# Expert attention: the next unit's keys projected right behind its queries, and rotated in front of the maxima of query tiles 2 and 3

## The reference

```python
q = (h @ wq + bq)   # 16 heads of 128; k and v likewise
q = q * cos + _rotate_half(q) * sin
k = k * cos + _rotate_half(k) * sin
scores = jnp.einsum('bhqd,bhkd->bhqk', q, k) / math.sqrt(HD)
scores = jnp.where(causal[None, None], scores, jnp.finfo(jnp.float32).min)
probs = jax.nn.softmax(scores.astype(jnp.float32), axis=-1).astype(q.dtype)
out = jnp.einsum('bhqk,bhkd->bhqd', probs, v)
```

## Time and profile before

| | |
|---|---|
| median of 3 runs | 2938.88 us (2935.98 to 2939.38) |
| the profiled execution | 2939.69 us |
| its span | 2937.9 us |
| mean granted TensorE clock | 0.93 |
| PE busy | 2447.8 us, 83% |
| DVE, ACT, POOL busy | 59%, 40%, 35% |

### The profile page before, as it was taken

One profiled execution on the slowest core, in us unless ns is written; L12 is line 12 of the kernel. 1 busy time (PEld: TensorE's weight loads), 2 busy tenths in 40 slices (PEclk: granted clock), 3 DMA queues, 4 the chain that ended last, 5 costly groups with the idle time before them and its releaser, 6 DMA issues. The chain is left out here.

```text
span 2937.9 us, 50913 instructions
## 1 busy us (share of the span) xinstructions
PE 2447.8 (83%) x18448; PEld 1669.7 (57%) x18448; DVE 1730.1 (59%) x3474; ACT 1184.5 (40%) x2881; POOL 1014.7 (35%) x1265
## 2 busy tenths in 40 slices
PE   6878778787787887878864999998979949999989
PEld 3467644676446774456742666667533336666675
DVE  4756667566685666846644766661356537666613
ACT  3643345344454434444422444440224514444401
POOL 0266521666215562146531444440040014444400
PEclk8999989999899998999977999999989979999989
DMA  2100001000010000000003000000010040000000
GB/s 49 40 2 2 2 15 33 2 2 2 8 36 5 2 2 8 18 6 2 2 1 102 17 16 16 11 5 1 2 42 1 1 102 18 16 16 11 5 0 15
DMA packets 74983, 46.64 MB, mean 16 GB/s; under 512 B 27416, under 2 KB 68256, under 8 KB 74400
## 3 DMA queue, kind: packets, MB, share of 16 engines
q1 hardware_dynamic: 74784, 43.95, 5.4%
HBM read 42.89 MB, written 1.05 MB: 15 GB/s over the span
## 5 line engine op out<-in xcount | busy, mean ns | idle before, releaser
L975 DVE SCALAR_TENSOR_TENSOR work<-four,taps_g,work 128x511 f32<-128x511 f32 (+2 forms) x384 | 284.2, 747 | 99.4 <-ACT work L751 89.2
L1365 POOL TENSOR_TENSOR rot<-q_plain,ropes 128x512 f32<-128x512 f32 x66 | 83.6, 1266 | 704.9 <-ACT q_plain L1387 704.9
L547 PE MATMUL four<-xT,wring 128*128 128x512 f32 x512 | 262.3, 640 | 11.9 <-issue 7.0
L1336 DVE TENSOR_REDUCE nmaxf<-four 128x1 f32<-128x512 f32 (+3 forms) x256 | 125.7, 491 | 165.5 <-PE four L1262 157.5
L1405 ACT ACTIVATE pr<-four,nmaxf 128x512 f32<-128x512 f32 (+3 forms) x256 | 133.9, 525 | 176.7 <-DVE nmaxf L1336 173.8
L1260 PE MATMUL four<-rot,rot 128*128 128x512 f32 (+3 forms) x512 | 189.7, 466 | 10.8 <-ACT oT L1200 5.6
L901 POOL TENSOR_TENSOR work<-work 128x256 f32<-128x256 f32 x184 | 120.3, 654 | 183.2 <-PE bank L634 91.4
L1368 POOL TENSOR_TENSOR rpart<-q_plain,ropes 64x512 f32<-64x512 f32 x132 | 167.3, 1268 | 10.3
L751 ACT ACTIVATE work<-four,taps_g 128x512 f32<-128x512 f32 x128 | 88.0, 688 | 187.9 <-PE four L547 187.9
L547 PEld LDWEIGHTS four<-xT,wring 128*128 128x128 f32 x512 | 99.6, 207 | 101.9 <-issue 95.7
L1281 PE MATMUL bank<-pT,vv 128*128 128x512 f32 (+3 forms) x512 | 149.4, 435 | 5.4 <-ACT pT L1411 5.4
(11 more groups left out here) (277 smaller groups left out, 5707.6 us busy)
## 6 DMA issues: line engine op xcount, KB each, us to landing
wqkv<-in_f_wq_dram SPq DMA_DIRECT2D x34, 128.0 KB, 2.2
wqkv<-in_f_wk_dram SPq DMA_DIRECT2D x34, 128.0 KB, 2.3
wqkv<-in_f_wv_dram SPq DMA_DIRECT2D x34, 128.0 KB, 2.3
wo<-in_f_wo_dram SPq DMA_DIRECT2D x2, 2048.0 KB, 11.3
we<-in_f_we_dram SPq DMA_DIRECT2D x4, 1024.0 KB
wring<-in_Ww_dram SPq DMA_DIRECT2D x4, 512.0 KB, 4.1
wring<-in_Wk_dram SPq DMA_DIRECT2D x4, 512.0 KB, 3.8
wring<-in_Wv_dram SPq DMA_DIRECT2D x4, 512.0 KB, 3.8
```

What stands on the lines that cost most here:

```text
L547: last = nc.tensor.matmul(k.bank[i % 3][:], wring[n % 2][:, c, h * P:(h + 1) * P], k.xT[:, c, b * T:(b + 1) * T], start=(c == 0), stop=(c ...
L975: ins = nc.vector.scalar_tensor_tensor(out=cbuf[i % 4][:, s:], in0=k.bank[i % 3][:, 0:T - s], scalar=taps_g[:, {"q": 0, "k": 1}.get(kind, ...
L1336: nc.vector.tensor_reduce(nmax[:, n:n + 1], k.bank[2 + i % 2][:, 0:(qt + 1) * P], AX.X, ALU.max, negate=True).then_inc(s_max, 1)
```

## The change

Three engines get another order inside a unit. On PE the key projection of the next unit moves from behind score tile 2 to directly behind the query projection. On DVE the rotation of those keys moves in front of maximum 2, and maximum 3 comes before scaling 2. On ACT the copies of turned tiles 0 and 1 move in front of exponentials 2 and 3. No instruction is added, taken away or resized, and the semaphores and the values waited for are the same.

```diff
@@ tensor engine, one unit
                             scores(u, 0)
                             scores(u, 1)
                             project(g, u + 1, 0)
+                            project(g, u + 1, 1)
                             scores(u, 2)
-                            project(g, u + 1, 1)
                             scores(u, 3)
@@ vector engine
                             maximum(u, 1)
                             normalise(u, 0)
                             normalise(u, 1)
+                            rope_k(g, u + 1)
                             maximum(u, 2)
+                            maximum(u, 3)
                             normalise(u, 2)
-                            maximum(u, 3)
-                            rope_k(g, u + 1)
                             normalise(u, 3)
@@ scalar engine
                             exps(u, 0)
                             exps(u, 1)
                             keep_q(g, u + 1)
+                            keep_p(u, 0)
+                            keep_p(u, 1)
                             exps(u, 2)
                             exps(u, 3)
-                            keep_p(u, 0)
-                            keep_p(u, 1)
```

## The result

The changed kernel takes 2957.66 us in the median (2954.47 to 2959.06, 4 runs), against 2939.13 us for the kernel before in the same session. The ratio is 1.0064, with a 95% interval of 1.0047 to 1.0081: 18.5 us slower. The forecast was 2948 us, 8.8 us slower, with a range of 2928 to 2965. Direction and mechanism held; the amount forecast was half of what came, and the time lies 1.7 us above the band of 2942 to 2956 that the forecast had given itself.

A forecast was written before the change was run, and what follows sets the result against it. TensorE, almost in balance with VectorE's chain to its last scaling, bounds the loop. Units 2 to 6 add 0.8 us, units 0, 1 and last 0.1 each: 1.1 per pass, 8.8 in all, giving 2948 us (range 2928 to 2965).

The forecast's parts named there:

- What bounds: Attention loop: TensorE 92.16 of 95.85 us per pass busy, almost in balance with VectorE's chain to its last scaling.
- TensorE's edit costs nothing: TensorE, key projection moved before score tile 2: same matmuls and weights, zero cost; score tile 2 comes 1.77 us later.
- ScalarE's edit costs nothing: ScalarE, two copies of turned probabilities moved before exponentials 2 and 3: they delay nothing, zero cost.
- The addition ends at 9.08 us, held by GpSimd's second half product: VectorE, key rotation's last addition: issued at 7.92 us into the unit, waits until 8.53, ends at 9.08.
- rival 1: VectorE's addition gets through before GpSimd's second half product: 1.2 us gained per pass, -9.5 us, 2929 us; chance 0.11.
- rival 2: GpSimd's own addition goes ahead of VectorE's waiting addition: unit 12.71 us, time 3034 us; chance 0.05.
- rival 4: VectorE's key rotation keeps its present 3.99 us wherever it lies: unit 11.86 us, time 2980 us; chance 0.08.
- Maximum 2 follows the addition by 0.03 us: VectorE, after the key rotation: maximum 2 at 9.11 us into the unit, 0.03 us after the addition's end.
- The term: VectorE's chain in units 2 to 6: next unit at 11.36 instead of 11.20 us, +0.16 us each, 0.8 per pass.
- Unit 0, unit 1 and the tail, 0.1 us each per pass: Attention loop pass: first unit paced by VectorE's chain, second slowed by the clock, last delayed; +0.1 us each.
- The clock: TensorE's clock after unit 0's stall: drops stay at 6 of 8 passes, 1.67 us each; bounds -10 to +17 us.
- rival 3: Clock behind unit 0: 2 drops instead of 6 pay for the change, -6.7 us, 2941 us; chance 0.16.

## Why the prediction was right, and where it was short

- *What bounds.* Right. TensorE and VectorE's chain were in near balance (unit 11.23 us, TensorE's own work 11.03; I had put 11.10), so any delay of the last scaling would show in full, and it did.
- *TensorE's edit costs nothing.* Right inside the change (with it 2957.7 us, without it 2954.9), for the reason that GpSimd hides it. The 2.8 us between the two times are within their intervals. Alone it costs 0.19 us per unit.
- *ScalarE's edit costs nothing.* Right, but I did not say what it is for: without it the change would be 25 us slower still, through the banks that transposes 2 and 3 need. That wait was missing from my list.
- *The addition ends at 9.08 us, held by GpSimd's second half product.* Right to 0.01 us, although the keys came at 5.44 and not at 5.62 (the wait for the port took up the difference), and rivals 1, 2 and 4 fell with it: unit distances were neither 11.1 nor 12.7 nor 11.86.
- *Maximum 2 follows the addition by 0.03 us.* Wrong, and this is the step that made the forecast half of the result. I took the 0.03 us from the earlier trace rows, where a reciprocal follows the addition. A maximum has a register instruction and its own waits in front of it, and all of them stood behind VectorE's wait for its own addition: 0.13 us in the 8 units 0, 0.19 us in 52 others, and 0.30 to 0.54 in the last 4, which come below. The term was +0.16 us per unit and measured +0.32; all steps behind it were right to 0.01 us (exponential +0.46, reciprocal +0.60, scaling +0.20, scaling of 256 columns 0.35 us, transposes and scores +0.53).
- *Unit 0, unit 1 and the tail, 0.1 us each per pass.* They measured 0.27, 0.3 and 0.37, in the main by the same gap. In all four passes of the second block the last unit with its tail lost another 0.6, 0.2, 0.2 and 0.2 us; there maximum 2 came 0.54, 0.31, 0.30 and 0.30 us behind the addition. With the own wait moved that gap is 0.03 us in these units as well, so this delay stood behind the own wait too; what makes it longer in these units stays open.
- *The clock.* I kept 6 drops, and the trace has 5. Of the 2 passes in which I saw no drop before, one had it earlier: in the first pass of the second block the clock was already low in unit 0, as it is in the changed kernel.

```profile
2407.14:2420.11 12.97, 10.87 (x46) 6.62 (x47) 8.24 (x16) 4.90 (x13) 5.07 (x4) 0.87 0.08 22
```

So rival 3 stood on one pass that had no low stretch, and not on two. That it could carry a result was a fair chance all the same: with the TensorE edit alone a clock that fell less often most likely hid the whole growth.

## What to carry to other kernels

When an instruction moves, take its register instructions and waits into account with it, and ask what they would stand behind: an engine's wait for its own last result keeps the preparation of the next instruction from running in its shadow. Price a gap by a row with the same successor, not by one with the same predecessor. And before reordering around a slow instruction, see whether it is slow: 1.66 us for an addition that takes 0.69 elsewhere was a conflict that one operand's place removed. That was worth 18 us in the units and 34 in the time, where neither the changed order nor any part of it tried here won anything.

## What was not expected of the hardware

A stall of 2.0 to 2.2 us on TensorE at the end of unit 0 is followed by a granted clock of 1.2 GHz in some passes and not in others of the same execution: 6 of 8 before, 5 of 8 after, 3 of 8 with the TensorE edit alone. With a stall of 1.6 us it was 1 of 16 passes (the changed kernel with the operand in PSUM, and the one without half products), and none where the stall was 1.1 us or filled. Each such drop cost 1.67 to 1.7 us, so 16 matmuls of no use made both kernels 9 to 11 us faster. When VectorE waits for the port while GpSimd has a further instruction to run, it gets its turn between the two: in the changed kernel the addition ended 0.55 us behind the half product, and GpSimd's next was held instead.
